# A four-layer graph network in one kernel: 128-column one-hot rows, a counts-only histogram, a later place for 57 gathers, and three wide matmuls more for each group of the attention sums

## The reference

```python
# layer 0: attention over incoming edges, one coefficient an edge
e = leaky_relu(concat(h[src], h[dst], emb_rel[etype]) @ attn_w1 @ attn_w2)
a = softmax of e over the edges of each dst
h_new = where(deg > 0, segment_sum(a * h[src], dst), h);  out = relu(h_new + h @ loop_weight)
# layer 1: sum of messages
out = relu(concat(h, segment_sum(h[col] @ W_msg + b_msg, row)) @ W_upd + b_upd)
# layer 2: two weighted hops, normed by the sum of the incoming weights
norm = maximum(segment_sum(w, dst), 1.0) ** -0.5
h = segment_sum((h * norm)[src] * w, dst) * norm          # twice; mean of the three h
# layer 3: graph attention with 8 heads and self loops, then a feed-forward part
alpha = softmax over dst of leaky_relu(a_src[src] + a_dst[dst]);  out = mean over heads of segment_sum(alpha * h[src], dst)
```

## Time and profile before

| | us |
|---|---|
| median of 3 runs | 5580.41 (5577.56 to 5592.24) |
| the profiled run | 5609.29 |
| its span in the trace | 5607.6 |
| busy: PE matmul, weight load | 2765.6, 2175.0 |
| busy: DVE, POOL, ACT | 2436.0, 1797.6, 473.0 |
| mean granted clock of TensorE | 0.614 |

### The profile page before, as it was taken

One profiled execution on the slowest core, in us unless ns is written; L12 is line 12 of the kernel. 1 busy time (PEld: TensorE's weight loads), 2 busy tenths in 40 slices (PEclk: granted clock), 3 DMA queues, 4 the chain that ended last, 5 costly groups with the idle time before them and its releaser, 6 DMA issues.

```text
span 5607.6 us, 46533 instructions
## 1 busy us (share of the span) xinstructions
PE 2765.6 (49%) x14416; PEld 2175.0 (39%) x14458; DVE 2436.0 (43%) x4207; ACT 473.0 (8%) x909; POOL 1797.6 (32%) x1742
## 2 busy tenths in 40 slices
PE   2085022122678885989898500004770001059995
PEld 1083000000157774979733400004660001059983
DVE  4068221111677776970101500006999800035565
ACT  0000000000022331003200100001220110000000
POOL 3705777777100001000000777771000077720000
PEclk8555555555555555989999655557995555555556
DMA  3102222222236665314476121110000123102210
GB/s 109 52 1 61 58 75 62 71 62 65 85 82 140 138 144 155 109 49 160 177 269 220 44 52 49 46 48 10 0 0 23 70 80 73 49 15 66 63 35 23
DMA packets 246489, 433.22 MB, mean 77 GB/s; under 512 B 140538, under 2 KB 142311, under 8 KB 231895
## 3 DMA queue, kind: packets, MB, share of 16 engines
q10 hardware_dynamic: 126001, 172.60, 12.0%
q1 hardware_dynamic: 64102, 198.46, 10.0%
q0 software_dynamic: 56256, 60.51, 5.8%
HBM read 280.32 MB, written 150.98 MB: 77 GB/s over the span
## 4 chain that ended last, share of the span: by engine, by line
PE 35%; issue 25%; another core or an unknown queue 17%; DVE 10%; POOL 9%; DMA 2%; ACT 1%; DVEq 0%; SPq 0%; ACTq 0%; POOLq 0%
POOL ring L652 8%; PE PS L1272 7%; PE PS L1196 5%; PE PS L1096 4%; PE PS L1098 4%; PE PS L989 3%; PE PS L1029 3%; PE PS L1167 3%; PE PS L992 2%; PE PS L1175 1%; DVE s_ring L1612 1%; DVE s_ring L1613 1%; PE PS L1270 1%; PE PS L1290 1%
## 5 line engine op out<-in xcount | busy, mean ns | idle before, releaser
L652 POOL DMA_INDIRECT ring<-d_h,idx_lin x1568 | 1579.1, 1007 | 598.6 <-issue 519.4
L1272 PE MATMUL PS<-arena,s_ring 128*128 x1968 | 432.5, 414 | 198.1 <-issue 198.1
L1096 PE MATMUL PS<-qa 128*125 128x150 bf16 x1050 | 412.3, 393 | 107.0 <-DVE arena L1662 46.1
L1929 DVE TENSOR_TENSOR big<-PS,big 128x800 f32<-128x800 f32 x196 | 193.8, 989 | 619.5 <-issue 335.7
L1272 PEld LDWEIGHTS PS<-arena,s_ring 128*128 128x128 f32 x1968 | 439.8, 330 | 9.2 <-issue 1.1
L1221 PE MATMUL PS<-big 128*125 128x128 bf16 x784 | 134.0, 300 | 618.5 <-issue 449.2
L1098 PE MATMUL PS<-qa 128*125 128x150 bf16 x1050 | 401.2, 382 | 0.0
L1059 PE MATMUL PS<-s_ring,arena 81*128 81x512 bf16 x196 | 121.6, 621 | 561.0 <-issue 353.3
L1221 PEld LDWEIGHTS PS<-big 128*125 128x125 bf16 x784 | 106.9, 209 | 664.8 <-issue 456.6
L671 POOL DMA_INDIRECT d_fa<-asd,start_i x25 | 50.2, 2010 | 889.5 <-DVEq L1323 882.2
L1231 PE MATMUL PS<-big,arena 125*128 125x200 bf16 x2352 | 271.6, 272 | 118.3 <-ACT arena L900 100.9
(11 more groups left out here) (445 smaller groups left out, 4572.2 us busy)
## 6 DMA issues: line engine op xcount, KB each, us to landing
big<-d_wgt SPq DMA_DIRECT2D x50, 1562.5 KB, 7.2
d_stash<-ring SPq DMA_DIRECT2D x196, 256.0 KB
arena<-d_stash ACTq DMA_DIRECT2D x196, 256.0 KB
big<-d_cnt SPq DMA_DIRECT2D x25, 1562.5 KB, 6.5
ring<-d_h,idx_lin POOLq DMA_INDIRECT x1568
d_cnt<-big ACTq DMA_DIRECT2D x13, 1562.5 KB, 5.5
d_wgt<-big ACTq DMA_DIRECT2D x13, 1562.5 KB, 15.7
d_cnt<-arena ACTq DMA_DIRECT2D x12, 1562.5 KB, 5.4
```

Source lines behind the costliest of these rows:

```text
L652: pool.indirect_dma_start(ring[:, HALF * h + s, :], None, table, bass.IndirectOffsetOnAxis(ap=idx_lin[:, CH * i + s:CH * i + s + 1], axis= ...
L1096: nc.tensor.matmul(bank(3 * half + s // 2, NP, 2 * CW, at), lhs, hot_step(half, s, W, 2 * CW), start=(s % 2 == 0), stop=False, skip_group_ ...
L1272: mm = nc.tensor.matmul(PS[:, bass.ds(place[s] + j % SUMS * BANK, D)], marks[:, j % 2, s, :], arena[:, bass.ds(at[s], D)], start=False, st ...
L1929: v_.tensor_tensor(picked.rearrange("p (s h k) -> p s h k", s=CB, h=H), free(PS[:, 0:1], [[BANK // 2, CB], [NB, H], [1, NB]], 2 * j * BANK ...
```

## The change

It has four parts.

1. `W` becomes 128, so that the one-hot rows of the histogram and of the dense blocks have 128 columns and PE loads all of them. The second look-up keeps 126 (`LKW`).
2. The histogram only counts: 25 moving columns, no product with the weights (DVE L1455 goes, and so does the split `w3`). The sums of weights come from elsewhere: SP stores the weights (`d_wl`) and loads them back as `w_edge` after the dense blocks; DVE scans them behind softmax0 (`scan_one`, with one more turn through PE); SP stores the scan (`d_wsum`); and POOL fetches each node's last value into `norm` with 25 gathers, for which DVE waits in layer 2.
3. POOL's order: the last 32 gathers of the first turn (chunks 94 to 97) go behind the fetch of layer 0's coefficient rows, and the 25 gathers of the own coefficients (L664) go from the middle of the second turn to its end. SP's stores follow.
4. In each attention step PE issues three wide matmuls of 512 columns on `ones_bf`, behind the 2nd, 4th and 6th product; nothing reads their result.

```diff
-    W = NP + 1
+    W = P
+    LKW = NP + 1
...
-        ROWS_AT, SELF_AT = 57, 70
+        ALPHA_AT = 94
+        ROWS_AT = 57
...
+            sp.dma_start(d_wl.rearrange("(p c) k -> p (c k)", p=P), w_lin).then_inc(S["dense_out"], 16)
...
+                    if turn == 0 and i == ALPHA_AT:
+                        sp.wait_ge(S["blk_ready"], NB)
+                        sp.wait_ge(S["dense_out"], 32)
+                        sp.wait_ge(S["fill_in"], 16)
+                        sp.dma_start(w_edge, d_wl.rearrange("(p c) k -> p (c k)", p=P)).then_inc(S["fill_in"], 16)
+                        sp.wait_ge(S["alpha_ready"], 1)
+                        sp.dma_start(d_al0.rearrange("(p c) k -> p (c k)", p=P), qa[:, 0:C]).then_inc(S["alpha_out"], 16)
...
+            sp.wait_ge(S["alpha_ready"], 2)
+            sp.dma_start(d_wsum.rearrange("(p c) k -> p (c k)", p=P), w_sum).then_inc(S["alpha_out"], 16)
...
-            tiles(0, d_h0, 40, NCH)
+            tiles(0, d_h0, 40, ALPHA_AT)
             pool.wait_ge(S["alpha_out"], 16)
             block_rows(d_al0, alpha0, "rows_in")
+            tiles(0, d_h0, ALPHA_AT, NCH)
...
+            pool.wait_ge(S["alpha_out"], 32)
+            for b in range(NB):
+                pool.indirect_dma_start(norm[:, b:b + 1], None, d_wsum, bass.IndirectOffsetOnAxis(ap=last_i[:, b:b + 1], axis=0),
+                                        bounds_check=EP - 1, oob_is_err=False).then_inc(S["nodes_in"], 16)
...
-            tiles(1, d_h3, ROWS_AT, SELF_AT)
+            tiles(1, d_h3, ROWS_AT, NCH)
             pool.wait_ge(S["nmx_ready"], 1)
             pool.wait_ge(S["scan_out"], 16)
             self_rows(d_sum3, packed(nmx, H))
-            tiles(1, d_h3, SELF_AT, NCH)
...
-                mm = nc.tensor.matmul(bank(7, NP, 4 * NB), free(s_bf[:, 0:1], [[HALF, NP]], h * W * HALF + s_),
-                                      free(h_bf[:, 0:1], [[HW * HALF, 4], [HALF, NB]], h * 4 * HW * HALF + s_),
+                mm = nc.tensor.matmul(bank(7, W, NB), free(s_bf[:, 0:1], [[HALF, W]], h * W * HALF + s_),
+                                      free(h_bf[:, 0:1], [[HALF, NB]], h * HW * HALF + s_),
...
-                    lhs = hot_step(half, s, 0, NP)
+                    lhs = hot_step(half, s, 0, W)
...
+                    if s % 2 and s < CH - 1:
+                        nc.tensor.matmul(bank(6, P, BANK), ones_bf[:, 0:P], free(ones_bf[:, 0:1], [[0, 2], [1, 2 * P]]), start=True, stop=True)
...
-            for j in range(3):
-                go(v_.tensor_copy(w3[:, j, :], w_lin))
-                if j < 2:
-                    go(v_.tensor_tensor(w_lin, w_lin, w3[:, j, :], ALU.subtract))
...
-                v_.tensor_tensor(free(h_bf[:, 0:1], [[HW * HALF, 3], [HALF, HW], [1, HALF]], (h * 4 + 1) * HW * HALF),
-                                 free(h_bf[:, 0:1], [[0, 3], [HALF, HW], [1, HALF]], h * 4 * HW * HALF),
-                                 w_at[:, :, :, c:c + HALF], ALU.mult).then_inc(S["hist_s"], 1)
...
             softmax0()
+            v.wait_ge(S["fill_in"], 32)
+            go(v_.memset(norm[:], 0.0))
+            scan_one(w_edge, w_sum, notst, cf_sum, SUMOP, 0.0)
+            mark("alpha_ready")
```

More of the change, by code:

```diff
@@ L587, in _ @@
             stash(1)
+            sp.wait_ge(S["nodes_in"], 16 * NB * 2)
+            sp.dma_start(d_self[0:N, :].rearrange("(b p) k -> p b k", p=NP), packed(nmx, H)).then_inc(S["self_out"], 16)
             sp.wait_ge(S["self_out"], 32)
@@ L1094, in part_products @@
                     at = s % 2 * (BANK // 2)
-                    lhs = hot_step(half, s, 0, NP)
-                    nc.tensor.matmul(bank(3 * half + s // 2, NP, 2 * CW, at), lhs, hot_step(half, s, W, 2 * CW),
+                    lhs = hot_step(half, s, 0, W)
+                    nc.tensor.matmul(bank(3 * half + s // 2, W, 2 * CW, at), lhs, hot_step(half, s, W, 2 * CW),
                                      start=(s % 2 == 0), stop=False, skip_group_check=True)
-                    mm = nc.tensor.matmul(bank(3 * half + s // 2, NP, 2 * CW, at + CW), lhs, hot_step(half, s, W + 2 * CW, 2 * CW),
+                    mm = nc.tensor.matmul(bank(3 * half + s // 2, W, 2 * CW, at + CW), lhs, hot_step(half, s, W + 2 * CW, 2 * CW),
                                           start=False, stop=False, skip_group_check=True)
@@ L1107, in overflow @@
                     pe.wait_ge(S["ov_used"], k + 1)
-                    nc.tensor.matmul(bank(OV_BANK, NP, 2 * CW), ov_hot[:, 0:NP], ov_hot[:, W:W + 2 * CW], start=True, stop=False, skip_group_check=True)
-                    nc.tensor.matmul(bank(OV_BANK, NP, 2 * CW, CW), ov_hot[:, 0:NP], ov_hot[:, W + 2 * CW:W + 4 * CW],
+                    nc.tensor.matmul(bank(OV_BANK, W, 2 * CW), ov_hot[:, 0:W], ov_hot[:, W:W + 2 * CW], start=True, stop=False, skip_group_check=True)
+                    nc.tensor.matmul(bank(OV_BANK, W, 2 * CW, CW), ov_hot[:, 0:W], ov_hot[:, W + 2 * CW:W + 4 * CW],
                                      start=False, stop=False, skip_group_check=True).then_inc(S["ov_mm"], 1)
@@ L1146, in _ @@
             chain(1, 1)
+            chain(1)
             pe.wait_ge(S["rows_in"], 16 * KG)
@@ L1220, in turn_hots @@
                 for s in range(CB):
-                    mm = nc.tensor.matmul(bank(4 + j, NP, P, s * P), free(look_hot[:, 0:1], [[CB, NP]], j * CB * W + s), ident_bf,
+                    mm = nc.tensor.matmul(bank(4 + j, NP, P, s * P), free(look_hot[:, 0:1], [[CB, NP]], j * CB * LKW + s), ident_bf,
                                           start=True, stop=True)
@@ L1446, in _ @@
             dhi_at = free(dhi_b[:, 0:1], [[0, HW], [1, C]])
-            w_at = free(w3[:, 0, 0:1], [[C, 3], [0, HW], [1, C]])
             iota_d = iota_h.rearrange("p (c s) -> p c s", s=HALF)
@@ L1479, in _ @@
             v.wait_ge(S["hist_used"], C + RING)
-            hist = bank(7, NP, 4 * NB)
+            hist = bank(7, NP, NB)
             go(v_.tensor_copy(deg[:], hist[:, 0:NB]))
-            go(v_.tensor_reduce(norm[:], hist[:, NB:4 * NB].rearrange("p (k b) -> p b k", b=NB), AX_X, ALU.add))
             mark("tri_in")
@@ L1909, in _ @@
                                 free(hi_b[:, 0:1], [[1, C], [0, NB]]), ALU.is_equal))
-            go(v_.tensor_copy(iota_look.rearrange("p (c s) -> p c s", s=CB), free(iota_row[:, 0:1], [[1, W], [0, CB]])))
+            go(v_.tensor_copy(iota_look.rearrange("p (c s) -> p c s", s=CB), free(iota_row[:, 0:1], [[1, LKW], [0, CB]])))
             go(v_.tensor_copy(ident_bf, ident[:]))
@@ L1917, in _ @@
                     go(v_.tensor_tensor(src_left, src_left, part, ALU.subtract))
-            at_look = free(lo_b[:, 0:1], [[0, W], [1, C]])
+            at_look = free(lo_b[:, 0:1], [[0, LKW], [1, C]])
             hi_look = free(hot_hi[:, 0:1], [[NB, C], [0, H], [1, NB]])
```

42 lines of the change are left out of this document (19 added, 23 removed).

## The result

The changed kernel takes 5616.8 us (median of 8 runs, 5605.8 to 5633.6) against 5579.0 for the kernel before (8 runs, 5571.4 to 5598.3): a ratio of 1.006, 95% interval 1.0045 to 1.0081. It is slower by 38 us; forecast were 120 us less. A repetition (7 runs) gave 1.007 (1.004 to 1.010).

What follows compares the result with a forecast made beforehand. No single engine bounds the whole; stages differ, and POOL's back-to-back gathers slow TensorE to 1.4 us a record. Terms −3 −75 −37 −22 +96 +3 −78 −5 sum to −121: 5460 us from 5580.4, 8-in-10 range 5360 to 5535.

Steps and rivals of the forecast that it cites:

- the attention's clock: Attention sums after the gathers: clock rises to 1.0, steps of 3.1 us for 3.84, −78 us.
- the rival of the slower side: Attention after the gathers: clock stays low, wide matmuls are only work, +102 instead of −78, 5645 us; chance 0.13.
- Histogram: Histogram after the gathers: fast strided loads let DVE set the pace, 0.97 us a group for 1.84, −75 us.
- The lower bound: Histogram with an unchanged load: fewer moving columns alone give 1.34 us a group, −43 us.
- First look-up: First look-up: 32 gathers leave it, so 45 us less under gathers, −37 us; 0 if their end doesn't free it.
- Dense blocks: Dense blocks: a matmul takes 0.13 us for 0.215, but store waits lengthen, −22 us; ends 0 and −139.
- Layer 0's sums: Layer 0's sums: POOL's moved gathers hold up TensorE until some 2320 us, 7 us a step meanwhile, +96 us.
- The norm's scan: Weights' sums (load, scan, store): under 12 us, hidden while PE and DVE wait for coefficient rows, 0.
- Attention under the gathers: Attention under POOL's gathers: 40 records a step for 34, 56 us for 48, one step fewer done, +3 us.
- Behind it: After the attention sums: PE's small matmuls run at full clock instead of 0.5, −5 us, between 0 and −10.

Runs made afterwards that it cites:

- the first four runs: The changed kernel without the three wide matmuls (0.965), with a fourth (0.976), with ones in the clearing matmul's stream (0.988), with POOL's order around layer 0 undone (0.998).

## Why the prediction was wrong

The step that failed is the attention's clock: "the clearing matmul and the three new ones are four to 16 records, the same ratio ... So I expect the clock to rise." It stayed at 0.5, the rival of the slower side, with steps of 4.69 us (forecast for that case: 4.75) and +105 us for −75. Had it risen as forecast, the attention would have taken 180 us less and the kernel would have been faster; with a real rise, in the kernel with a fourth wide matmul, it is 0.978 of before for 1.006, some 155 us less. What the runs show is this: with the clearing matmul and three wide ones to 16 records the clock stays down, whether the clearing matmul has zeros in both operands, ones streaming, or ones as weights (three kernels); with the clearing matmul and four wide ones, five in all, it rises (on both kinds of chip). Why layer 0's four are enough and these four aren't stays open. It may be the clearing matmul, which starts a bank that other products then add to; it may be that four are short in this stage whatever they are, with its 128 weight columns for 125. A step with four wide matmuls and no clearing one wasn't tried. The zeros alone don't tell the stages apart, since in layer 0 one of zeros in four was no hindrance.

The comparison with layer 0 was weaker than it looked in another way. There, in the same code, the clock rose 14 us after PE had its full work in the kernel before, 15 and 7 in the two profiled runs of the changed one, but 52 us after it with the norm gathers late and 110 in the kernel without wide matmuls in the attention. One trace had shown me a quick case, and "the same ratio" had no margin on record.

By its other steps:

- *Histogram*, −90 for −75. Right that DVE would set the pace and that strided rows load fast too; 0.85 us a group for 0.97, since the records of DVE's two instructions overlap: (1.84 − 0.85) x 86 = 85, and 5 us more that I can't place. The lower bound was wrong: I added the moving columns to the load (−43 without a fast load), and the run with 125 columns gives −2. Without the 128 columns there is no gain. The Trainium skill, "TensorE: Matmul & The Clock Gate", section "Weight-path perf modes — Fast Weight Load (FWL) and DoubleRow", says that the fast load covers strided rows and that about 2x was measured: this trace agrees, 326 to 164 ns.
- *First look-up*, −39 for −37 (−35 by the repetition). *Dense blocks*, −11 for −22. There a matmul takes 434/2072 = 0.210 us, not 0.13: loads fell from 250 to 128 ns, but 150 columns took as long as before. I had taken the longer of load and columns as the pace (0.125 us); it is more than either.
- *Layer 0's sums*, +77 for +96: right in kind, too large in size. 6.7 us a step under the gathers for 7; but the standstill set in only at 2081 us, 6 us after the first step and 21 us after the first gather at 2060, and DVE's steps came quick again 2 us after POOL's last gather, not 20. A late clock adds to the stage in some runs.
- *The norm's scan* was hidden, as said: layer 0 began 4 us earlier relative to the dense blocks.
- *Attention under the gathers*: steps of 56 us, as said. *Behind it*, −11 for −5.
- *Second look-up*, −22, not forecast. In ten other runs with the changed kernel's code there, on the chips of this kind, it took 1065 to 1076 us, and 1085 in the kernel before with rows of 128 columns. So some 10 us of it come with the change, by what isn't known, and the rest is spread between runs.

The sum of the stages comes to −2 and the medians to +38: the profiled run of the kernel before was slower than all eight that were timed, and that of the changed kernel faster than its median. By the medians, the wide matmuls cost 98 us, and without them the change is worth 60 us (0.989); with the norm gathers late as well it would be more, as they cost 40. So one term decided the sign.

## What to carry to other kernels

Matmuls that only lift the clock need an experiment with one more and one fewer, because one too few pays the whole price and gets nothing: here three cost 98 us against none, and four saved some 60 (0.978 of before for 0.989, on two chips). When a load is to become shorter, ask what streams beside it. With loads of 325 ns a matmul took 0.230 us, whether 25 or 100 columns streamed; with loads of 128 to 148 ns it took 0.198 us with 100 columns and 0.210 with 150, more than load or columns alone. Neither the sum nor the longer of the two fits all three, so measure the pair. And move background gathers only after pricing what lies under them at the new place, not only at the old.

## What the runs showed of the hardware

**Chips differ in what gathers do to TensorE.** On three chips, and in the result, the long stages under POOL's gathers ran at about 1.4 us a TensorE record. It takes time to set in: 21 us in layer 0's sums, and softmax0's short turns, beside 53 us of gathers, weren't held up at all. On the chip of the first four runs the dense blocks ran under gathers at full pace (the row from 700 us of the kernel with ones in the stream: 3741 records and 342 gathers in 480 us, 0.128 us a record; without gathers, in the changed kernel's row from 1475 us, 4142 records in 530 us, also 0.128). The kernel before took 3787 us there and 5579 to 5602 on the others. So a third of this kernel's time is a standstill that the other chip doesn't have, and the order of POOL's queue has opposite signs on the two: moving the 32 and the 25 gathers back saved 48 us on one and cost 38 on the other. What makes the chips differ, or whether it is something that comes and goes with time, no run shows.

**Whether the data of a matmul matters to the clock stays open.** In the attention a clearing matmul with zeros as weights, as stream or as both left the clock at 0.5, and a further wide matmul of ones, the fifth of its size in a step, lifted it. In layer 0's sums one of zeros in four didn't prevent the rise, which came after about 45 us, within what the unedited code shows there (7 to 110). So nothing here shows that zeros count for less. A fourth wide matmul of zeros in the attention, beside the clearing one, would tell the data from the number, and wasn't tried.
